# Cross attention of a decoder layer: value products of two key tiles together, behind steps 11 and 3, with 14 slots for exponentials

## The reference, cut to what matters

```python
# B, S, D = 4, 512, 512; the context is 512 rows of 256; 32 heads of 16
q = (x @ Wq).reshape(b, n, N_HEADS, HEAD_DIM)
k, v = jnp.split(ctx @ Wkv, 2, axis=-1)
q = apply_axial_rope(q, pos_map)
k = apply_axial_rope(k, ctx_pos_map)
logits = jnp.einsum('bqhd,bkhd->bhqk', q, k) * scale
w = jax.nn.softmax(logits, axis=-1)
attn = jnp.einsum('bhqk,bkhd->bqhd', w, v)
return attn.reshape(b, n, N_HEADS * HEAD_DIM) @ Wout + bout
```

## Time and profile before

| | |
|---|---|
| median of 3 runs | 2136.97 us |
| profiled execution | 2134.5 us, its span 2132.7 us |
| granted TensorE clock, mean | 0.965 |
| TensorE matmuls, busy | 1982.2 us, 93% |
| TensorE weight loads, busy | 1385.6 us, 65% |
| VectorE, busy | 1356.2 us, 64% |
| ScalarE, busy | 1046.5 us, 49% |
| exponentials of the cross core (L1339) | 512 of 599 ns |
| reductions of the cross core (L1389) | 248 of 1211 ns |
| value products of the cross core (L1233) | 1024 records of 612 ns |

### The profile page before, as it was taken

One profiled execution on the slowest core, in us unless ns is written; L12 is line 12 of the kernel. 1 busy time (PEld: TensorE's weight loads), 2 busy tenths in 40 slices (PEclk: granted clock), 3 DMA queues, 4 the chain that ended last, 5 costly groups with the idle time before them and its releaser, 6 DMA issues. The chain is left out here.

```text
span 2132.7 us, 32709 instructions
## 1 busy us (share of the span) xinstructions
PE 1982.2 (93%) x10991; PEld 1385.6 (65%) x10991; DVE 1356.2 (64%) x2805; ACT 1046.5 (49%) x1890; POOL 706.1 (33%) x610
## 2 busy tenths in 40 slices
PE   7998999968789999998899899998999999999998
PEld 6875666656533334343777566666787888787876
DVE  6455666557689897976778566645331325577775
ACT  3424554445368676865443455534322221476775
POOL 0003655436512332323466465531000000143433
PEclk9998999989889999999999799998999999999999
DMA  5637676247665545443474867626120206434342
GB/s 202 223 141 183 149 170 153 91 163 268 233 180 119 141 113 140 119 104 95 188 242 181 203 153 164 149 81 245 45 99 1 79 25 254 171 67 76 64 77 37
DMA packets 151994, 297.75 MB, mean 140 GB/s; under 512 B 24722, under 2 KB 43284, under 8 KB 150740
## 3 DMA queue, kind: packets, MB, share of 16 engines
q1 hardware_dynamic: 114052, 242.29, 38.1%
q10 hardware_dynamic: 29040, 34.74, 6.0%
q0 software_dynamic: 8736, 18.62, 4.8%
HBM read 181.55 MB, written 102.50 MB: 133 GB/s over the span
## 5 line engine op out<-in xcount | busy, mean ns | idle before, releaser
L1339 ACT ACTIVATE cross_c_prob<-bank 128x512 f32<-128x512 f32 x512 | 271.1, 599 | 116.7 <-PE bank L1192 115.4
L1389 DVE TENSOR_REDUCE row_max<-bank 128x2 f32<-128x1024 f32 x248 | 290.6, 1211 | 27.6 <-PE bank L1158 26.6
L1859 PE MATMUL bank<-moe_hT,moe_w 128*128 128x512 f32 x1056 | 250.1, 393 | 7.7 <-DVE moe_w L2148 7.7
L1192 PE MATMUL bank<-stack 56*128 56x512 f32 (+4 forms) x768 | 232.9, 428 | 7.0 <-ACT cross_c_prob L1339 3.1
L1859 PEld LDWEIGHTS bank<-moe_hT,moe_w 128*128 128x128 f32 x1056 | 199.1, 189 | 50.1 <-issue 8.1
L1158 PE MATMUL bank<-stack 48*128 48x512 f32 (+4 forms) x720 | 190.7, 443 | 25.6 <-PEq L71 13.7
L1192 PEld LDWEIGHTS bank<-stack 56*128 56x128 f32 (+1 forms) x768 | 118.5, 193 | 136.4 <-ACT cross_c_prob L1339 69.6
L1339 ACT ACTIVATE first_c_prob<-bank 128x512 f32<-128x512 f32 (+3 forms) x256 | 106.1, 436 | 120.1 <-PE bank L1195 117.1
L1339 ACT ACTIVATE rotary_c_prob<-bank 128x512 f32<-128x512 f32 (+3 forms) x256 | 105.6, 436 | 117.8 <-PE bank L1195 115.2
L1385 DVE CUSTOM_DVE_ANT_0 first_c_masked<-bank,later 128x128 f32<-128x128 f32 (+3 forms) x240 | 108.8, 485 | 77.8 <-PE bank L1158 77.1
L1158 PEld LDWEIGHTS bank<-stack 48*128 48x128 f32 (+1 forms) x720 | 93.3, 196 | 98.4 <-DVE row_max L1389 45.1
(11 more groups left out here) (402 smaller groups left out, 4482.6 us busy)
## 6 DMA issues: line engine op xcount, KB each, us to landing
qk_parts<-first_p_parts SPq DMA_DIRECT2D x32, 512.0 KB, 2.6
stack<-qk_parts SPq DMA_DIRECT2D x64, 256.0 KB, 6.4
qk_parts<-cross_p_parts SPq DMA_DIRECT2D x32, 512.0 KB, 2.6
stack<-qk_parts SPq DMA_DIRECT2D x256, 64.0 KB, 2.6
qk_parts<-rotary_p_parts SPq DMA_DIRECT2D x32, 512.0 KB, 2.7
moe_gate_up_e<-in_experts_gate_up SPq DMA_DIRECT2D x8, 1408.0 KB, 9.1
moe_raw<-in_shared_packed SPq DMA_DIRECT2D x11, 768.0 KB, 8.5
stack<-qk_parts SPq DMA_DIRECT2D x16, 512.0 KB, 5.3
```

Of the source, the lines that this page charges most:

```text
L1192: last = nc.tensor.matmul(bank[:, 0 : S - q0], k_stack[slot][r : r + ALL_ROWS, at, m * P : (m + 1) * P], q_stack[slot][r : r + ALL_ROWS, a ...
L1339: nc.scalar.activation(probability(g, step // HEADS_AT_ONCE, step % HEADS_AT_ONCE), psum[bank_at["score", n]][:, 0 : S - q0], ACT.Exp).the ...
L1389: nc.vector.tensor_reduce(row_max[:, g % 2, m, j - 1 : j + 1], c.banks[:, first : first + WIDE, :], AX_X, ALU.max).then_inc(s.max_done, 1)
L1859: last = nc.tensor.matmul(psum[bank][:], weights(pa, f, k), hT[p % 2][:, pb, k, :], start=m == 0, stop=m == len(steps) - 1)
```

## The change

The value products of the cross core come two tiles at a time: tiles 0 and 1 behind step 11 of their group, tiles 2 and 3 behind step 3 of the next one. `values_behind` returns a list, and the two loops that call it run over that list. The ring of exponentials has 14 slots in place of 8; the slot of an exponential and ScalarE's wait for it are worked out from `PROB_SLOTS` as before. The other two attentions get a list of at most one tile, at the same steps as before.

```diff
--- before.py
+++ after.py
@@ -31,7 +31,7 @@
 LOWEST = -3.0e38
 HEADS_AT_ONCE = 4
 STACK_SLOTS = 4
-PROB_SLOTS = 8
+PROB_SLOTS = 14
 MAX_ROW = 96
 STACK_ROWS = MAX_ROW + 2 * HEADS_AT_ONCE
 
@@ -982,6 +982,7 @@
         start_k = lambda m: m * P if causal else 0
         WIDE = HALVES
         VALUES_LAG, SUMS_STEP = 7 if cross else 9, 4
+        VALUES_AT = {11: (0, (0, 1)), 3: (1, (2, 3))}
         bank_score, bank_shared = ((0, 1, 2, 3), (4, 5, 7)) if cross else ((0, 1, 2), (3, 4, 7))
         bank_o, bank_sum = (6, 6) if cross else (5, 6)
         N_SCORE = len(bank_score)
@@ -1002,8 +1003,11 @@
 
         def values_behind(g, step):
 
+            if cross:
+                back, tiles = VALUES_AT.get(step, (0, ()))
+                return [(g - back, m) for m in tiles if g >= back]
             n, beat = divmod(g * N16 + step - VALUES_LAG, HEADS_AT_ONCE)
-            return divmod(n, TT) if beat == 0 and 0 <= n < GROUPS * TT else None
+            return [divmod(n, TT)] if beat == 0 and 0 <= n < GROUPS * TT else []
 
         def probability(g, m, j):
 
@@ -1283,8 +1287,7 @@
                             scoresT(g, step)
                             if step == MAX_STEP and g + 1 < GROUPS:
                                 max_transpose(g + 1)
-                            if values_behind(g, step):
-                                g_v, m_v = values_behind(g, step)
+                            for g_v, m_v in values_behind(g, step):
                                 values(g_v, m_v)
                                 if causal and g_v == GROUPS - 1:
                                     sums_at_end(m_v)
@@ -1295,8 +1298,7 @@
                             if projected_at(g, step):
                                 project(*projected_at(g, step))
                     for step in range(VALUES_LAG):
-                        if values_behind(GROUPS, step):
-                            g_v, m_v = values_behind(GROUPS, step)
+                        for g_v, m_v in values_behind(GROUPS, step):
                             if causal:
                                 sums_at_end(m_v)
                             values(g_v, m_v)
```

## The result

The changed kernel takes 2185.41 us (median of 4 runs, 2182.89 to 2187.96), the kernel before 2138.72 us in the same comparison (4 runs, 2126.91 to 2142.66). The ratio is 1.0228, with a 95% interval of 1.0185 to 1.0271. The forecast was 2155, from 2139 to 2168: right in sign, too small, and the time lies outside the range. The profiled execution after took 2184.24 us, with a span of 2182.5; its mean granted clock of TensorE is 0.951, where it was 0.965 before.

A forecast was written before the change was run, and what follows sets the result against it. The prediction took VectorE to bound plain groups, in lock step with TensorE. Plain groups 13.6, projection groups 3.6 and the last two groups 1.5 us sum to 18.7, giving a median of 2155 us, range 2139 to 2168.

The forecast's parts named there:

- The joined block: Value products of two tiles on end in TensorE's queue: 1.85 us, bounded by 1.74 and 1.98.
- The rival in which the blocks do not join: Two tiles' blocks take 1.98 instead of 1.85 us, adding 7 us: 2162, counted within the forecast's range.
- Sites 1 and 2: Blocks at step 3 (site 1) and step 11 (site 2): VectorE loses 0.59 us at each in a plain group.
- What is given back at step 15: With no block at step 15, VectorE's wait of 0.24 us goes; 0.33 us back per plain group.
- Plain and projection groups: Cross core groups without and with a projection: 0.85 us more in each of 16, 0.30 in each of 12.
- The order as a whole: Moving the value products in TensorE's queue costs 18.7 us over the whole cross core.
- The last two groups: Groups 30 and 31 of the cross core, bound by TensorE and ScalarE: together 1.5 us more.
- The ring: 14 slots for exponentials cost nothing, since ScalarE's wait for a slot is met before the score it needs.
- The gain on TensorE (2117): Rival, chance 0.08: TensorE sets the pace and 20 us saved by joinings are kept, giving 2117 us.
- The rival with half of the loss hidden: One of the two places with a joined block does not cost: about 2145 us, chance 0.14.
- 2170 by a late ScalarE: Rival, chance 0.10: ScalarE becomes a second bound, 0.7 us beyond its slack in 28 groups, adding some 14 us.

The follow-up runs named there:

- e2_join01: Changed kernel with only tiles 0 and 1 joined behind step 11; tiles 2 and 3 stay apart at steps 15 and 3; ratio to the kernel before 1.0057.
- e6_repeat: Changed kernel with the transposed score products of steps 14, 15, 0 and 1 issued twice into the same bank; ratio to the kernel before 1.0086.
- e5_join23: Changed kernel with only tiles 2 and 3 joined, at step 3; tiles 0 and 1 apart at steps 7 and 11; ratio to the kernel before 1.0237.
- e1_slots14: Kernel before, its order kept, with only the ring enlarged to 14 slots; 2131.82 us against 2132.07, ratio 1.0003.
- e3_refill: Changed kernel plus tile 2's value products made once more at step 15 and thrown away; 2172.93 us, ratio to the kernel before 1.0164.
- e7_refill7: Changed kernel plus tile 0's value products made once more at step 7 and thrown away; 2211.01 us, ratio to the kernel before 1.0333.
- e4_leave15: Order of the kernel before with 14 slots, tile 2's value products left out, so step 15 is empty; 2142.89 us, ratio to the kernel before 1.0031.

## Why the prediction was right on the order and missed the clock

**The step that failed** is a sentence of the first part: "The granted clock of TensorE is 1.00 throughout, the 2.4 GHz level, so no term below changes for it." It was true of the kernel before from group 1 on (group 0 ran mostly at 0.50, in the first row below, as it does after the change) and was carried over to the kernel after, whose order of TensorE's work is what the change is about. In the kernel after the clock falls to the 1.2 GHz level another 22 times in the cross core, for about the length of a slow joined block, and each fall costs 1.6 us: 35 us that no term and no rival held. So the range could not hold the time either.

```profile
591.62:604.00 12.38, 11.30 (x42) 4.19 (x42) 7.93 (x7) 7.00 (x13) 0.42 (x2) 0.50 0.49 112
604.00:643.20 39.20, 35.44 (x228) 13.23 (x224) 36.58 (x39) 30.69 (x60) 9.17 (x15) 1.00 0.65 170
```

**The joined block,** taken as 1.85 us, is 1.85 wherever the clock is 1.00. The rival in which the blocks do not join is out.

**Sites 1 and 2,** 0.59 us each: e2_join01 has site 2 alone and loses 0.58 in a plain group. In e6_repeat both waits lie where they were put, 0.35 ahead of the flip and 0.52 later. What is given back at step 15 shows in that no wait of VectorE ahead of A0 is left in group 8, and in e2_join01, where that block stays and 0.24 us of wait is left with it. But e5_join23 shows that the terms do not simply add: site 1 alone costs 0.5 net and not 0.26.

**Plain and projection groups,** 11.75 and 14.8: 11.74 and 14.73 without a fall. The order as a whole, 18.7 us: 18.4 in e6_repeat. That they lie so close is in part luck, since the interval of that ratio alone reaches from 12 to 25 us and the run has falls outside the 26 groups; inside them the order costs 14.4 where 15.5 was forecast.

**The last two groups,** 1.5 us, took 28.65 - 20.81 = 7.8 more; four falls, put at 1.6 each, are 6.4 of that, and 1.4 is left for the term. No run shows these two groups of the changed order without a fall and without added work.

**The ring,** put at nothing, costs nothing (e1_slots14).

**The other rivals.** The gain on TensorE (2117) did not come: B0's scores are waited for, as their place in the queue had it. The rival with half of the loss hidden fell with sites 1 and 2. The one nearest in time, 2170 by a late ScalarE, was wrong in its mechanism: in group 8 VectorE reads C0 at 710.81 without a wait.

**What is shown.** In groups 4 to 29 the stretch of scores without a block brings the falls: e3_refill and e6_repeat fill it and have none, e7_refill7 fills another and has 18. A wait for a DMA is not what they need: 14 of the 16 falls of the changed kernel have none ahead. e4_leave15 and e5_join23 fit this with 8 and 12 falls, but TensorE also waits for DMAs there.

**What stays open.** Which groups fall is not settled. Groups 6 and 8 have the same work ahead of the block, yet one falls and the other doesn't, and the granted clock of e5_join23 differs from run to run. Nor did a run show why the stretch between steps 3 and 11, which has no value block either, but the transposes of the maxima, so seldom brings a fall: none of the 16, one in e2_join01, and two of the four in the last two groups. And e6_repeat has falls in groups 2 and 3, so a filled stretch alone is not enough there.

## What to carry to other kernels

Price a block of matmuls at both levels of the clock before moving work out of TensorE's queue: the stretch that it leaves may no longer hold the clock, and whatever runs next pays. Look for the longest stretch that the new order leaves without its dense work, and compare it with what stands there now, rather than take the clock from the trace of before. And hold the length of a joined block against what the engine behind it has in store: here that was two reductions, so all that the longer block took beyond them became a wait.

## What the runs showed of the hardware

In group 6 TensorE's clock fell though no wait of its matmuls longer than 0.32 us preceded it and the records have TensorE busy for 3.48 of 3.88 us. Busy time in the records is thus by itself no sign that the clock will hold. Work that the result does not need was worth more than it cost: e3_refill does 208 more matmul records in 26 groups than the change and is 13.6 us shorter there, and e6_repeat does 104 more and is 26.2 us shorter.
